# A gated cross-attention and mixture-of-experts block: the expert products summed over high and low weight halves in one 256-column region, with one vector sum per expert in place of two

## The reference, cut to what matters

```
h = silu(a) * b,   (a, b) = split(flat @ w1.T)          # 512 hidden values a token
for e in range(8):
    routed = routed + h * w_se[:, e:e + 1] @ w2[e].T    # w_se is zero but for the 2 chosen experts
x = x + tanh(g_ffn) * (shared + routed)
```

## Time and profile before

| | us |
|---|---|
| median of 3 runs | 1189.57 |
| lowest and highest | 1183.27, 1192.06 |
| the profiled execution, its own time | 1187.66 |
| its span, first to last instruction | 1185.5 |
| busy PE, PEld | 1125.9, 900.3 |
| busy DVE, ACT, POOL | 803.0, 470.8, 445.8 |

### The profile page before, as it was taken

How to read it: one execution, slowest core, us unless ns; L and a number is a source line. 1 busy time by engine, 2 the same in 40 slices (tenths; PEclk the granted TensorE clock), 3 DMA queues, 4 the chain that set the end, 5 groups by cost and what they waited for, 6 DMA issues and landing times.

```text
span 1185.5 us, 22353 instructions
## 1 busy us (share of the span) xinstructions
PE 1125.9 (95%) x7475; PEld 900.3 (76%) x7475; DVE 803.0 (68%) x1777; ACT 470.8 (40%) x723; POOL 445.8 (38%) x583
## 2 busy tenths in 40 slices
PE   3879999999999999999999899999999899999997
PEld 1557877777777777777787687788888788888886
DVE  5456687677676676786776776547544488777776
ACT  4455555545545546545555442224222111111111
POOL 2122335235236236235245323300000566666564
PEclk9979999999999999999999999999999899999999
DMA  7977566647647647656664511478653454554452
GB/s 145 234 124 144 118 106 136 134 87 148 138 106 120 140 103 124 141 113 111 133 125 69 130 38 44 168 228 265 213 181 124 150 161 144 170 160 148 148 159 77
DMA packets 115377, 163.16 MB, mean 138 GB/s; under 512 B 38044, under 2 KB 79934, under 8 KB 115264
## 3 DMA queue, kind: packets, MB, share of 16 engines
q1 hardware_dynamic: 103492, 123.71, 46.2%
q0 software_dynamic: 11776, 38.03, 10.6%
HBM read 75.24 MB, written 52.10 MB: 107 GB/s over the span
## 4 chain that ended last, share of the span: by engine, by line
PE 75%; issue 10%; DVE 7%; POOL 4%; DMA 2%; ACT 1%; POOLq 0%; another core or an unknown queue 0%; DVEq 0%; ACTq 0%
PE ps L743 15%; PE ps L790 11%; PE ps L688 10%; PE ps L792 6%; PE ps L705 6%; PE ps L596 4%; PE ps L608 3%; PE ps L639 3%; PE ps L568 3%; PE ps L563 3%; PE ps L775 3%; PE ps L617 1%; PE ps L591 1%; PE ps L662 1%; PE ps L673 1%
## 5 line engine op out<-in xcount | busy, mean ns | idle before, releaser
L790 PE MATMUL ps<-regr,gh 128*128 x600 | 222.1, 407 | 1.1 <-DVE ot L1298 0.7
L873 ACT ACTIVATE Pt<-ps,pbias 77x1024 f32<-77x1024 f32 x128 | 141.5, 1106 | 181.4 <-PE ps L596 168.2
L792 PE MATMUL ps<-regr,gl 128*128 x600 | 170.1, 284 | 0.0
L790 PEld LDWEIGHTS ps<-regr,gh 128*128 128x128 f32 x600 | 114.0, 190 | 25.4 <-issue 2.2
L1170 DVE TENSOR_REDUCE mneg<-ps 128x8 f32<-128x616 f32 x128 | 101.5, 794 | 46.6 <-PE ps L568 42.8
L963 ACT ACTIVATE gh<-ps 128x512 fp32r<-128x512 f32 x75 | 44.8, 599 | 208.3 <-PE ps L775 108.0
L792 PEld LDWEIGHTS ps<-regr,gl 128*128 128x128 f32 x600 | 114.2, 190 | 0.0
L1418 POOL TENSOR_TENSOR x<-x,regf 128x512 f32<-128x512 f32 x32 | 41.2, 1288 | 193.0 <-DMA x<-in_x 193.0
L688 PE MATMUL ps<-x2h,winh 128*128 128x512 f32 x256 | 110.7, 432 | 0.5 <-DVE OHR L1078 0.5
L1353 POOL TENSOR_TENSOR gl<-gf,gh 128x512 fp32r<-128x512 f32 x64 | 82.7, 1294 | 62.3 <-ACT gh L830 62.2
L688 PE MATMUL ps<-x2h,winl 128*128 128x512 f32 x256 | 100.8, 394 | 0.0
(11 more groups left out here) (200 smaller groups left out, 2567.8 us busy)
## 6 DMA issues: line engine op xcount, KB each, us to landing
regr<-regr SPq DMA_DIRECT2D x96, 256.0 KB, 5.9
y_dram<-Pt SPq DMA_DIRECT2D x64, 256.0 KB, 2.2
regf<-in_x SPq DMA_DIRECT2D x32, 256.0 KB, 2.8
x<-in_x SPq DMA_DIRECT2D x32, 256.0 KB, 7.0
y_dram<-res SPq DMA_DIRECT2D x32, 256.0 KB
regr<-regr SPq DMA_DIRECT2D x96, 77.0 KB, 4.7
x_dram<-x2h SPq DMA_DIRECT2D x14, 512.0 KB, 2.9
x_dram<-x2l SPq DMA_DIRECT2D x14, 512.0 KB, 3.7
```

The lines of the kernel that those rows point to most:

```text
L790: e.matmul(o, gh2[:, k % 3, fc, :], w2v[:, bass.ds(val, 1), fc, :, :].rearrange("p o h d -> p (o h) d"), start=fc == 0, stop=False, skip_g ...
L792: m = e.matmul(o[:, 0, :], gl2[:, k % 3, fc, :], w2v[:, bass.ds(val, 1), fc, 0, :].rearrange("p o d -> p (o d)"), start=False, stop=fc == ...
L873: e.activation(Pt[0:K, 4 * k:4 * k + 4, :].rearrange("k (n j) t -> k n (j t)", n=2), bank_of["sc", b, k][0:K, :, :], ACT.Exp, bias=pbias[: ...
```

## The change

In `experts`, each quarter fc has three matmuls of 256 columns (high x high, low x high, high x low) in place of one of 512 and one of 256, and all go into columns 0 to 255 of the bank. In `vector`, one `scalar_tensor_tensor` an expert reads these columns. The semaphore `acc0` goes, and `acc1` counts as before.

```diff
                     if n == 0:
                         e.wait_ge(s["gl2"], k + 1)
-                    o = bk[:, :].rearrange("p (h d) -> p h d", h=2)
+
                     for fc in range(4):
-                        e.matmul(o, gh2[:, k % 3, fc, :], w2v[:, bass.ds(val, 1), fc, :, :].rearrange("p o h d -> p (o h) d"),
-                                 start=fc == 0, stop=False, skip_group_check=True)
-                        m = e.matmul(o[:, 0, :], gl2[:, k % 3, fc, :], w2v[:, bass.ds(val, 1), fc, 0, :].rearrange("p o d -> p (o d)"),
-                                     start=False, stop=fc == 3, skip_group_check=True)
+                        for n_, (g2, d) in enumerate(((gh2, 0), (gl2, 0), (gh2, 1))):
+                            m = e.matmul(bk[:, 0:D], g2[:, k % 3, fc, :], w2v[:, bass.ds(val, 1), fc, d, :].rearrange("p o d -> p (o d)"),
+                                         start=fc == 0 and n_ == 0, stop=fc == 3 and n_ == 2)
                     m.then_inc(s["ex"], 1)
```

```diff
                 for n in range(2):
-                    v = bank_of["ex", k, n][:, :].rearrange("p (h d) -> p h d", h=2)
                     e.wait_ge(s["ex"], 2 * k + n + 1)
                     if n:
                         e.wait_ge(s["acc1"], 2 * k + 1)
-                    e.scalar_tensor_tensor(ot[:, o, :], v[:, 0, :], rt[:, k, 1 + n:2 + n],
-                                           ot[:, o, :] if n else yt[k % RY][:, 2 * D:3 * D], ALU.mult, ALU.add).then_inc(s["acc0"], 1)
-                    e.wait_ge(s["acc0"], 2 * k + n + 1)
-                    e.scalar_tensor_tensor(ot[:, o, :], v[:, 1, :], rt[:, k, 1 + n:2 + n], ot[:, o, :],
-                                           ALU.mult, ALU.add).then_inc(s["acc1"], 1)
+                    e.scalar_tensor_tensor(ot[:, o, :], bank_of["ex", k, n][:, 0:D], rt[:, k, 1 + n:2 + n],
+                                           ot[:, o, :] if n else yt[k % RY][:, 2 * D:3 * D], ALU.mult, ALU.add).then_inc(s["acc1"], 1)
```

## The result

The changed kernel takes 1219.33 us (median of 4 runs, 1215.33 to 1222.17), the one before 1188.0 beside it: ratio 1.026, interval 1.0233 to 1.0287. The forecast was 1212 in a range of 1192 to 1224, slower at 0.66. The direction, the mechanism and the range held; the loss is 31 us where the sum said 22 and the forecast, set against 1188.0, 24.

A forecast was written before the change was run, and what follows sets the result against it. PE bounds the kernel before; after the change its sequencer was to set the pace. +24.6 - 1.7 - 0.5 - 0.3 = +22.1 on the profiled 1187.66 gives 1209.8, about 1212 on the median; range 1192 to 1224.

The forecast's parts named there:

- PE bounds, with 3.247 a tile, and the sequencer is ahead with 0.55 us to spare: Expert stage before the change: PE takes 3.247 us a tile, its sequencer needs 2.70, so 0.55 us is spare.
- Two register instructions a quarter, 1200 in all: PE's sequencer: the third matmul's low-half weights need another address, so 1200 register instructions in the stage instead of 600.
- 0.11 us a step: Sequencer time per added register instruction, 0.11 us; eight a tile add 0.88, giving 3.58 us a tile and +24.6 us.
- 3.5 to 3.65: Sign that the forecast is right: a tile of the changed kernel takes 3.5 to 3.65 us.
- case B: Sequencer binds at another step price: 0.09 gives 1200 (chance 0.05); upper bounds 0.13 and 2.77 give 1229 (above 1224: 0.04).
- +0.010 for three matmuls against the pair: PE's columns: three 256-column matmuls take 0.360 us against 0.350; +0.08 a tile, +5.9 us, beneath the sequencer's term, not added.
- rival A: PE stays the bound, the second address costing the sequencer 0.07 us or less: +3.7, 1193; chance 0.26 together with D.
- -1.7 and -0.5 for DVE: Two of four DVE sums go: PE's 1.7 us of waits vanish, and the final scatter starts 0.52 us earlier.
- -0.3 for the start: Half clock at stage start: PE is slower than the sequencer, so about one tile escapes its +0.33 us.
- Gathers cost nothing more: Gather issue, five tiles ahead: longer tiles give more time, the one 0.7 us wait grows no longer; nothing counted.
- C (a faster pace): 256-column matmuls run at their columns' time alone, 0.110 us: tile 3.09, total 1176; chance 0.03.
- D (DVE): PE's order hides more bank waits, so DVE's 0.97 us a tile matters: no less than 1192; chance 0.26 together with rival A.

## Why the prediction was right, and where its sum was short

- *PE bounds, with 3.247 a tile, and the sequencer is ahead with 0.55 us to spare:* right. The runs with four and six further instructions put the edge between 0.50 and 0.74 us of further work. The sequencer's own time was taken as 2.70; the tiles with six and eight further instructions give 3.435 - 6 x 0.124 = 2.69, 3.661 - 8 x 0.124 = 2.67, and the changed kernel 3.684 - 8 x 0.124 = 2.69.
- *Two register instructions a quarter, 1200 in all:* right, counted.
- *0.11 us a step:* this is the term that was mis-sized, though the range took it in. I took the step of the earlier trace rows and took off something for the load and matmul that don't follow. The trace after has 0.124 whatever follows, 3.684 a tile and not 3.58, and so just above the 3.5 to 3.65 that was named as the sign. That is 0.104 x 74 = +7.7 us of the 9 that the sum lacked. The step of the row itself, with nothing taken off, was the right price. The upper end of case B, 1229, took 0.13 and 2.77, and was too dear by both.
- *+0.010 for three matmuls against the pair:* somewhat dear. With one address a tile takes 3.287, +0.040 and not +0.080. Eight times 0.005 in place of 0.010: three matmuls take about 0.355 there, not the 0.360 of line 705. It had no effect on the forecast, because the sequencer's time lies above it; it would have been the whole result in rival A (measured +2.8 us where A has +3.7). My +5.9 was twice the 3.0 us of that run.
- *-1.7 and -0.5 for DVE:* no measured time shows them; the runs with and without the second sum differ by less than their intervals. As far as the traces go, the waits behind the 1.7 belonged to one execution: the traces with four, six and eight further register instructions have DVE's four sums too, and none has a wait of PE for them between 930 and 1180 us. So there was nothing to win back; with the 7.7 that is about what the sum lacked. The way from the start of the last matmul to the end of the span went from 7.3 to 7.1 us, less than the 0.5 counted; in the run of the kernel before with one sum it is 1181.9 - 1175.1 = 6.8, which has the 0.5.
- *-0.3 for the start:* no run separates this term. A lead of 2.1 us would have lasted some five tiles at 0.44 each, but there was none of that size: in the trace after, narrow windows have the wait of line 787 passed at 937.23 for tile 1 and at 943.35 for tile 2, and their first matmuls start at 938.67 and 943.57. The lead is 1.44 us, then 0.22, and stays there; between the two lies the wait for the low half, 0.9 us.
- *Gathers cost nothing more:* right. With 3.684 a tile from tile 3 to tile 68, within 0.01 of what the sequencer's own time and its steps make (2.70 + 0.99), nothing is left for a late one.
- The profiled execution's span is 33.2 us longer than that of before (1218.7 against 1185.5). 31.0 of it lie between the first and the last matmul of the experts (932.7 to 1211.6 against 930.3 to 1178.2), with one wait among them that the run with the second sum put back doesn't have: 0.9 us at 943.6, for a low half of the first tiles. Another 2.4 are there before the stage begins, where no instruction has changed: the granted clock of the first 100 us was 0.74 in this execution and 0.93 in that of before; that this is the cause isn't shown. The end gave 0.2 back.
- *The rivals:* A (PE stays the bound) fell with the count of 1200 and the tile of 3.684, and came true where one address was taken away. B (the sequencer binds, at another price) had the mechanism and missed the step on both sides. C (a faster pace) fell with 0.12 between the starts. D (DVE) fell with the two runs on the sums.

## What to carry to other kernels

In this kernel a matmul whose operand address comes from a register was not only columns and a weight load: each new address was an instruction of the sequencer, 0.124 us of its time, about as much as the 0.120 between two matmuls of 256 columns. Cutting a matmul at the same columns into more pieces with more addresses turned an engine bound by its columns, 3.247 us a tile, into one bound by its sequencer, 3.684, and the loss started where the sequencer's time passed the engine's own: nothing measurable at 3.20, 1.2% at 3.44 and 2.6% at 3.69. So add up the sequencer's instructions of a loop from a place where it catches up after a wait, and compare that with the engine's own time before work is split; a busy time of 49.1 of 50 us didn't say which of the two binds.

## What was not expected

- One load and one matmul behind a register instruction cost the sequencer as much as two of each (both steps lie between 0.122 and 0.126); no run shows why.
- Giving the range of the read number was cheaper here than leaving it out: without it there is a check for each matmul, 21 sequencer instructions a call in place of 10, and +140 us (one run).
- PE's busy time hid a bound sequencer: 49.1 of 50 us with 12% fewer tiles done. The count of matmuls in the window, not the busy time, shows it.
